# VectorE's order of sums and scans in a tick of a selective-scan decoder block

## The reference, cut to what matters

```python
def _selective_scan(u, delta, A, Bm, Cm, D):
    def step(s, inp):
        d_t, B_t, C_t, u_t = inp
        dA = jnp.exp(d_t[..., None] * A)
        dBu = d_t[..., None] * B_t[:, None, :] * u_t[..., None]
        s = s * dA + dBu
        y = jnp.einsum('bds,bs->bd', s, C_t)
        return (s, y)
...
x = _layernorm(x + mixer(x))              # norm, in_proj, conv, silu, selective scan, gate, out_proj, + x
x = _layernorm(x + cross_attention(x, ctx, ctx))   # rope, softmax over 2*64 keys, W_o, norm, relu(W_ffn)
x = _layernorm(x + experts(x))            # top 2 of 8 experts by softmax, silu(x W1 + b1) * (x W3 + b3) W2, and a shared expert
```

## Time and profile before

| | |
|---|---|
| median of 3 runs | 1158.65 us (1152.01 to 1164.36) |
| the profiled execution's own time | 1159.1 us |
| its span | 1157.2 us, from 11 us to the end: 1.9 us lie around it |
| mean granted TensorE clock | 0.832 |
| PE busy | 893.1 us (77%) |
| DVE busy | 822.3 us (71%) |
| POOL, ACT busy | 540.2 us (47%), 532.0 us (46%) |
| bodies 1, 2, 3 | about 250, 252 and 252 us each; DVE busy 204.5, 206.1 and 205.2 us of it |
| body 4, the second stage alone | 213 us, DVE busy 55.8 us |

### The profile page before, as it was taken

How to read it: one execution, slowest core, us unless ns; L and a number is a source line. 1 busy time by engine, 2 the same in 40 slices (tenths; PEclk the granted TensorE clock), 3 DMA queues, 4 the chain that set the end, 5 groups by cost and what they waited for, 6 DMA issues and landing times.

```text
span 1157.2 us, 13851 instructions
## 1 busy us (share of the span) xinstructions
PE 893.1 (77%) x3960; PEld 674.2 (58%) x3960; DVE 822.3 (71%) x1239; ACT 532.0 (46%) x1011; POOL 540.2 (47%) x335
## 2 busy tenths in 40 slices
PE   4845558858779999676788999577698975867996
PEld 2434445347568785265667874265487862645885
DVE  1699997568999966579989954599999851213233
ACT  3533452644455535554546516465456422313442
POOL 1256650274458840463667830754487713002552
PEclk9955558868779999788789999698799996755998
DMA  6110101101124311101023302101033212001330
GB/s 204 38 37 37 55 1 37 74 19 64 38 74 127 87 43 57 74 37 65 28 97 114 95 16 91 47 29 66 26 128 110 73 46 82 0 1 46 103 116 29
DMA packets 38255, 72.62 MB, mean 63 GB/s; under 512 B 3871, under 2 KB 12712, under 8 KB 38174
## 3 DMA queue, kind: packets, MB, share of 16 engines
q1 hardware_dynamic: 38174, 71.65, 19.3%
HBM read 65.14 MB, written 2.30 MB: 58 GB/s over the span
## 4 chain that ended last, share of the span: by engine, by line
PE 43%; issue 20%; DVE 19%; POOL 11%; ACT 5%; DVEq 1%; POOLq 0%; ACTq 0%
PE ps L893 9%; DVE hs L1075 7%; PE ps L970 6%; POOL dbu L534 6%; PE ps L749 6%; PE ps L828 5%; PE ps L867 4%; DVE yacc L1125 3%; DVE work L1223 3%; PE ps L822 2%; PE ps L912 2%; PE ps L937 2%; POOL work L572 2%; POOL work L554 2%; PE ps L807 2%
## 5 line engine op out<-in xcount | busy, mean ns | idle before, releaser
L534 POOL TENSOR_TENSOR dbu<-v,bbc 128x1024 f32<-128x1024 f32 x128 | 303.1, 2374 | 214.1 <-DVE v L1061 116.3
L1075 DVE TENSOR_TENSOR_SCAN hs<-ps,carry,dbu 128x512 f32<-128x512 f32 x256 | 313.2, 1267 | 1.8 <-ACT ps L643 1.0
L643 ACT ACTIVATE ps<-delta,neg_a 128x512 f32<-128x512 f32 x256 | 175.5, 692 | 209.9 <-DVE hs L1075 209.4
L749 PE MATMUL ps<-ident,hs 128*128 128x128 f32 x1024 | 179.2, 332 | 92.3 <-DVE yacc L1125 77.7
L749 PEld LDWEIGHTS ps<-ident,hs 128*128 128x128 f32 x1024 | 152.1, 174 | 120.0 <-DVE hs L1075 74.6
L1125 DVE SCALAR_TENSOR_TENSOR yacc<-ps,ctok,yacc 128x512 f32<-128x512 f32 x240 | 167.5, 739 | 1.2 <-PE ps L749 1.0
L564 POOL TENSOR_TENSOR w_lo<-w13s,w_hi 128x512 fp32r<-128x512 f32 x72 | 92.9, 1290 | 126.0 <-ACT w_hi L724 124.1
L970 PE MATMUL ps<-w2s,work 128*128 128x256 f32 x576 | 136.3, 380 | 0.3
L893 PE MATMUL ps<-x_hi,w_hi 128*128 128x512 f32 x288 | 108.1, 457 | 10.7 <-DVE work L1229 10.3
L970 PEld LDWEIGHTS ps<-w2s,work 128*128 128x128 f32 x576 | 105.8, 190 | 14.9 <-DVE work L1229 1.5
L737 ACT ACTIVATE work<-ps,half_b 128x512 f32<-128x512 f32 x72 | 49.5, 688 | 141.0 <-PE ps L893 131.4
(11 more groups left out here) (167 smaller groups left out, 1211.8 us busy)
## 6 DMA issues: line engine op xcount, KB each, us to landing
w13s<-in_w SPq DMA_DIRECT2D x72, 256.0 KB, 2.8
bbc<-brow_dram SPq DMA_DIRECT2D x32, 512.0 KB, 3.9
w2s<-in_w SPq DMA_DIRECT2D x36, 256.0 KB, 2.7
cbc<-comb_dram SPq DMA_DIRECT2D x32, 256.0 KB, 3.6
work<-work SPq DMA_DIRECT2D x16, 256.0 KB, 2.3
xn<-in_x SPq DMA_DIRECT2D x5, 512.0 KB, 4.7
xt<-in_x SPq DMA_DIRECT2D x4, 512.0 KB, 3.6
rope<-in_rope_q SPq DMA_DIRECT2D x4, 512.0 KB, 4.2
```

Source lines behind the costliest of these rows:

```text
L534: pool.tensor_tensor(dbu[:, i % DRING, :, :], v[:, 2 * h:2 * h + 2, :], bbc[:, n // 2 % 2, n % 2, :].rearrange("p (o t) -> p o t", o=1) .t ...
L643: act.activation(ps[:, unit % 2, :], delta[:, q, :], ACT.Exp, scale=neg_a[:, q * NS + m:q * NS + m + 1]).then_inc(da_done.sem, 1)
L749: last = pe.transpose(ps[:, bank, t * P:(t + 1) * P], src(t), ident[:, :])
L1075: dve.tensor_tensor_scan(hs[:, m % 2, q, 0:TC], ps[:, unit % 2, :], dbu[:, n % DRING, q % 2, :], carry[:, m, q:q + 1], ALU.mult, ALU.add). ...
```

## The change

In `schedule()` a scan tick's entries become sum, mid, scan, sum2, scan2, late. Only DVE reacts to "sum2" and "scan2": its two sums and two scans are no longer sum, sum, scan, scan but sum, scan, sum, scan. Its "mid" part, which stood behind both sums and ahead of both scans, now stands behind the first sum. Its "late" part still stands behind the last scan. The instructions are the same ones, with the same operands and waits; the other engines' streams keep their order.

```diff
     for s in range(SCAN_TICKS):
         t = PRE_TICKS + s
-        steps += [("early", t), ("sum", s), ("mid", t), ("scan", s), ("late", t)]
+        steps += [("early", t), ("sum", s), ("mid", t), ("scan", s), ("sum2", s), ("scan2", s), ("late", t)]
...
-                if kind == "sum" and 3 <= n < 2 * NS + 3:
-                    sum_states(j, *divmod(n - 3, 2))
-                if kind == "scan":
-                    for unit in range(2 * n, min(2 * n + 2, NS * Q)):
+                if kind in ("sum", "sum2") and 3 <= n < 2 * NS + 3:
+                    sum_states(j, *divmod(n - 3, 2), kind == "sum2")
+                if kind in ("scan", "scan2"):
+                    unit = 2 * n + (kind == "scan2")
+                    if unit < NS * Q:
                         m, q = divmod(unit, Q)
...
-            def sum_states(j, n, half):
-
-                for t in range(2 * half, 2 * half + 2):
-                    c = ctok[:, t, n:n + 1]
-                    dve.wait_ge(*ht_ps.at(j, n * NT + t + 1))
+            def sum_states(j, n, half, odd):
+
+                t = 2 * half + odd
+                c = ctok[:, t, n:n + 1]
+                dve.wait_ge(*ht_ps.at(j, n * NT + t + 1))
...
```

More of the change, by code:

```diff
@@ L1112, in convolution @@
                         done += 1
-            def sum_states(j, n, half):
-                for t in range(2 * half, 2 * half + 2):
-                    c = ctok[:, t, n:n + 1]
-                    dve.wait_ge(*ht_ps.at(j, n * NT + t + 1))
[L1119 to L1126, removed]
+            def sum_states(j, n, half, odd):
+                t = 2 * half + odd
+                c = ctok[:, t, n:n + 1]
+                dve.wait_ge(*ht_ps.at(j, n * NT + t + 1))
+                if n == 0:
+                    dve.wait_ge(*ctok_done.at(j, 1))
+                    dve.wait_ge(*xz_ps.at(j, 2 * Q))
+                    dve.tensor_scalar(yacc[:, t, :], ps[:, 2 + t % 2, :], c, None, ALU.mult).then_inc(y_done.sem, 1)
+                else:
+                    dve.wait_ge(*y_done.at(j, (n - 1) * NT + t + 1))
+                    dve.scalar_tensor_tensor(out=yacc[:, t, :], in0=ps[:, 2 + t % 2, :], scalar=c,
+                                             in1=yacc[:, t, :], op0=ALU.mult, op1=ALU.add).then_inc(y_done.sem, 1)
             def row_stats(j, k, src, t, before):
```

## The result

The changed kernel takes 1202.78 us (median of 4 runs, 1201.51 to 1222.53), the kernel before 1157.74 us beside it on the same chip: a ratio of 1.038, 95% interval 1.0326 to 1.0433. The longest run, 1222.53 us, was in a slower state at a lower clock (0.759), and the ratio leaves it out. That is slower, as forecast, but just outside the range of 1167 to 1200: the loss is 43 to 45 us, not 25. The profiled execution's span went from 1157.2 to 1200.6 us, and the mean granted TensorE clock from 0.832 to 0.801.

The account below looks back on a forecast made before the run. VectorE was taken as full in body 0 and still busiest in bodies 1 to 3, waiting at some "mid" parts. Losses of 7.9 us a body, 23.6 for three, plus 1.0 for expert ticks, on 1159.1 gave 1184 us; range 1167 to 1200.

Parts of the forecast that it names:

- the mechanism: Bodies 1 to 3: sum done behind "mid" waits, 0.65 us each; TensorE's late part queued behind a later second transpose group.
- Body 0 and the expert ticks: Body 0: tick stays 3.67 us; expert ticks: later transposes set TensorE back 0.3 us a body, 1.0 us in all.
- the race of gm and dbu: VectorE's gm against POOL's dbu: shifted starts give plus or minus 6 us; gain bringing time within 1%, chance 0.05.
- the kernel got no faster: Rival, attention ticks: "mid" starts 0.65 us sooner, saving 15.6 us, giving 1143; chance 0.05.
- TensorE had no room: Rival: TensorE swallows the transposes' delay, leaving only sums behind waits, 7.8 to 11.7 us, 1167 to 1171; chance 0.14.
- t = 6, 8, 10: 3 x 0.65: Attention loop, bodies 1 to 3: a sum behind rec's wait lengthens each tick 0.65 us, 1.95 us a body.
- TensorE's clock falls: Rival: attention loops of bodies 2 and 3 fall to body 1's lower clock, 9.7 us more, 1194; chance 0.08.
- 12: t = 11 and 12: value product and rec 0.83 us later, plus 0.65 of sum: 1.48 us a body.
- 14: t = 13 and 14: output product 1.05 us later, plus the sum behind xa: 1.70 us a body.
- 15 to 18: Forecast for t = 15 to 17: feed-forward product and relu 1.0 us later, plus 0.65 of sum: 1.35 us a body.
- 19, 20: Gate products end later, so top two waits 0.75 us, with 0.65 of sum behind it: 1.40 us a body.
- What would show it: Changed profile's signs: rec waits 1.3 us, longer waits before xa, relu, top two, more TensorE idle, bodies of 260 us.

Follow-up runs that it names:

- experiment 4: The change, with TensorE's first group of transposes at t = 6, 8, 10, 12 of bodies 1 to 3 made four times over (the fill): 1181.1 us.
- experiment 7: The kernel before, with TensorE's first group of transposes at t = 6, 8, 10, 12 of bodies 1 to 3 made four times over: 1152.91 us.
- experiment 1: Against the change, VectorE's second sum directly behind "mid", ahead of both scans (sum, mid, sum, scan, scan): 1174.8 us, ratio 1.0146.
- experiment 2: Against the change, VectorE's "mid" behind both sums, sums and scans alternating (sum, scan, sum, mid, scan): 1160.56 us, ratio 1.0012.
- experiment 6: Against the change, VectorE's second sum behind both scans (sum, mid, scan, scan, sum): 1258.42 us, ratio 1.086.
- experiment 3: The change, with TensorE's "late" part ahead of its second group of transposes: 1180.09 us, ratio 1.0213.

## Why the prediction was wrong in size

**The direction held, and the mechanism for about half of the loss.** Body 0 and the expert ticks lost nothing (forecast: 0, and 0.3 a body; t = 24 to 33 are equal to 0.07 us, but for one, 0.36 shorter). gm's mean went from 1.117 to 1.150 us, within the tenth allowed, so the race of gm and dbu was at most a small part of it (2.3 us over the 72). Another meeting with dbu was a part, and a gain: VectorE's conversion of top two's indices (CAST, L1261), which took 1.69 us beside a dbu of POOL before, now takes 0.17, and from top two's first step to the next scan it is 3.24 us and not 4.44, in all three bodies. No rival on the other side came: the kernel got no faster, and TensorE had no room.

**The step that failed** is "t = 6, 8, 10: 3 x 0.65". At t = 6, with t = 5, it was 0.64. At t = 8 and 10 it was 3.64 us each in body 2. The sum was worked out at the durations of the kernel before, that is, at the clock that TensorE had then, and with ScalarE's exponential as what frees ont. With the clock up (experiment 4) both are so, and the ticks are 0.66 longer. In the change itself TensorE ran at 1.2 GHz from the second group to the end of the scores. Against experiment 4, rec to ont takes 1.13 us more (5.59 and 4.46), since the second group (0.76 and 0.63) and two further sets of transposes (1.91 and 1.04, 0.63 and 0.38) now stand on the path, and the scores 1.78 more (3.75 and 1.97): 2.91 of the 2.98 between the loops of 14.22 and 11.24.

**The rival that came true was given 0.08 and half its price.** "TensorE's clock falls" was put at 1.6 us in 3 ticks of 2 bodies, since body 1 was counted as low already: 9.7. The runs give 20.4 (330.4 less 310.0). The 1.6 was the loop's price in the old order (12.20 less 10.58), where of TensorE's work only the scores are on the path. In the new order it is 2.98: 2 ticks, 3 bodies, less the 1.5 that t = 10 of body 3 was spared, and 0.4 more at t = 10 of body 1, make 16.7; t = 12 (0.7, 0.7 and 0.3) and t = 14 of body 2 (1.8) bring it to 20.3. The rule of the Trainium skill named there (TensorE: Matmul & The Clock Gate, "HAM oscillation — how this bites in real kernels") had the direction right: the mean granted clock fell from 0.832 to 0.801. And a view was at hand that should have raised the chance: in body 1 the old loop had already fallen to the lower clock with a wait of 1.94 us ahead of the scores, and the change adds waits in all three bodies.

**The other terms**, forecast for a body, and measured in bodies 1, 2, 3:

| ticks | forecast | the change | with the fill |
|---|---|---|---|
| 12 | 1.48 | 2.1, 2.1, 1.7 | 1.4, 1.4, 1.4 |
| 14 | 1.70 | 2.3, 2.1, 2.2 | 2.3, 0.3, 2.2 |
| 15 to 18 | 1.35 | 1.0, 1.5, 2.2 | 1.2, 2.0, 1.5 |
| 19, 20 | 1.40 | 2.1, 2.1, 2.1 | 2.1, 2.1, 2.1 |
| 22 | 0 | 0.4, -0.9, -0.5 | 0.5, -0.7, 0.0 |

At t = 14 the output product began 3.52 us after the sums' start, where the forecast had 3.59; but from there to xa it was 3.10 us and not the 2.65 of the earlier trace rows, since the lower clock lasted through the product behind it. At t = 20 the gate products were timed at the 1.89 us of before; they took 3.4 at the lower clock, and top two waited 2.58 us, not 0.7; 1.2 us of that came back in top two itself, by the CAST. Both are the same error again, and the fill, which ends at t = 12, doesn't mend the second.

With the fill the change loses 6.1, 7.1 and 8.7 us a body, 21.9, where the forecast had 23.6. That is close, but partly by luck: against the old order with the same fill (experiment 7) it loses 28 us (1181.1 and 1152.91; in the scan ticks of the two traces 10.2, 7.7 and 10.3 a body), since body 1 of before had itself been at the lower clock in two ticks. So the forecast's sum was short by some 4 us even without the clock in the loop.

**What would show it**: rec's wait was to be 1.3 us and was 0.93 to 1.01, since xa, which had no wait in this loop of body 2, now waits ahead of it for the output product: with the fill 0.28 and 0.20 us, which with rec's 0.93 and 1.02 makes the forecast's 1.2 to 1.3. In the change itself xa waits 1.15 and 0.53, and mx 2.00 and 2.54 for the scores. The waits before xa and relu, and TensorE's grown idle time ahead of the transposes, came, the one before xa at 2.23 us where 1 was written.

**Open**: why the clock falls in just this loop. The second sum stands behind "mid" in experiment 1 and behind a scan in experiment 2, and in neither did the loop fall to the lower clock; in the change it stands behind both. That is no rule either: in experiment 6 it also stands behind both, and the scores ran at the upper clock, while in experiment 3 those at t = 9 of bodies 2 and 3 were slow (2.92 and 3.02 us). Nor does the longest wait alone tell the two apart: the old loop had one of 2.25 us ahead of the scores of body 2 and kept the upper clock, the change has one of 2.22. Shown is that filling TensorE's waits brings the clock back; what decides was not tried apart.

## What to carry to other kernels

On an engine that works in order, put the work whose inputs are ready ahead of the place where it waits: 0.65 us moved behind a wait cost 0.65 us in the loop, and a scan moved ahead of it won up to 0.77 (6.91 to 6.14), as long as nobody waits for what the delayed place puts out. Look then at what is queued, on its own engine, behind the instruction that the moved work releases: moving the same sum one scan further back cost another 56 us (1202.78 to 1258.42), part of it by TensorE's queue and its clock, and some 12 us in body 0, where the next scan waits for the same transposes. And where a change makes TensorE wait more often, work out its path at both levels of the clock, with all its instructions that the change puts there, before giving the lower level a chance and a price.

## What the runs showed of the hardware

Useless work made the kernel faster. With 48 redundant transposes a body the mean granted clock went from 0.801 to 0.83, TensorE's busy time from 934.8 to 922.0 us, and the time down by 22 us; in the kernel before, by some 4.5 us (ratio 0.9961, interval 0.9932 to 0.9991).

The same loop has two steady lengths by the clock: 10.58 or 12.20 us in the old order, 11.24 or 14.22 in the new, and it changed over within a body (t = 10 of body 3: 9.04 instead of 10.55). A profile of one body at one level says little of what the next will do.
